# Layer 1's neighbour sums: 26 groups of sixteen chunks and two scattered quartets per half group, in place of 21 groups and three quartets

## What is computed

```
row, col = (edge_index[0], edge_index[1])          # row = src, col = dst
agg = segment_sum(x[col], row, num_segments=3125)
h = (1.0 + eps) * x + agg
h = h @ W1.T + b1
... batch normalisation over the nodes, ReLU ...
return h @ W2.T + b2
```

## Time and profile before

| | |
|---|---|
| median of the runs | 7078.2 us |
| span of the profiled execution | 8961.2 us (27% above the median) |
| TensorE matmul busy in the span | 5673.7 us (63%) |
| VectorE busy | 4867.9 us (54%) |
| GpSimd busy | 4865.9 us (54%) |
| ScalarE busy | 1151.3 us (13%) |
| mean granted TensorE clock | 0.674 of full |
| stage that the change touches | 4725 to 5720 us of the span |

### The profile page before, as it was taken

The page is one execution under the profiler, slowest core; times in us unless marked ns, Lnnn a source line. Parts: engine busy times, 40 slices in busy tenths (PEclk is TensorE's granted clock), DMA queues, the critical chain, the costliest instruction groups (busy, mean ns, idle before and its releaser), DMA issues. The chain is left out here.

```text
span 8961.2 us, 134318 instructions
## 1 busy us (share of the span) xinstructions
PE 5673.7 (63%) x28658; PEld 4800.1 (54%) x28659; DVE 4867.9 (54%) x17338; ACT 1151.3 (13%) x3238; POOL 4865.9 (54%) x4715
## 2 busy tenths in 40 slices
PE   6555556677777767777768778656666665333334
PEld 5555555466666556666655555456666663333333
DVE  6555554455555545555557777545555553444555
ACT  1111111111111111111112222100000001000001
POOL 2566564555555355555527888445454451566664
PEclk6555555777777877777779999865655556555556
DMA  5334434333333233333324444333333332333332
GB/s 154 95 95 97 94 94 126 92 97 93 95 93 96 57 102 94 94 97 98 94 53 67 69 69 69 78 83 88 89 89 87 89 89 37 77 75 75 74 77 49
DMA packets 930244, 770.85 MB, mean 86 GB/s; under 512 B 586631, under 2 KB 762899, under 8 KB 928115
## 3 DMA queue, kind: packets, MB, share of 16 engines
q0 software_dynamic: 245936, 426.87, 19.9%
q1 hardware_dynamic: 675276, 329.60, 14.6%
q10 hardware_dynamic: 8960, 13.52, 0.6%
HBM read 681.88 MB, written 86.32 MB: 86 GB/s over the span
## 5 line engine op out<-in xcount | busy, mean ns | idle before, releaser
L1180 POOL DMA_INDIRECT there<-table_wide,idx x1664 | 1597.4, 960 | 1396.8 <-DVE prod L1203 615.9
L1271 PE MATMUL ps<-here,hot_t 128*128 x3328 | 1238.1, 507 | 631.3 <-DVE there L1222 599.7
L2288 POOL DMA_INDIRECT there<-table_wide,idx x832 | 792.7, 953 | 902.6 <-DVE msg L2364 434.8
L1222 DVE TENSOR_TENSOR there<-there,ps 128x512 f32<-128x512 f32 x832 | 571.2, 687 | 1169.8 <-remote 607.7
L1271 PEld LDWEIGHTS ps<-here,hot_t 128*128 128x128 f32 x3328 | 740.9, 247 | 756.5 <-issue 668.9
L2677 POOL DMA_INDIRECT there<-table_narrow,idx x832 | 791.3, 951 | 649.5 <-issue 259.1
L693 POOL DMA_INDIRECT rec<-out_recd,posd x806 | 817.5, 1014 | 564.4 <-issue 263.9
L1279 PE MATMUL ps<-relu,hot_s 128*128 128x128 f32 x3328 | 878.0, 356 | 140.3 <-DVE hot_s L1211 108.1
L2837 PE MATMUL ps<-here,hot_t 128*128 x1664 | 434.5, 436 | 803.6 <-DVE prod L2758 419.3
L1947 POOL DMA_INDIRECT partial_sums<-row_sums1a,idx1a x504 | 814.9, 1617 | 167.4 <-issue 147.3
L1279 PEld LDWEIGHTS ps<-relu,hot_s 128*128 128x128 f32 x3328 | 688.5, 238 | 326.3 <-issue 272.1
(11 more groups left out here) (486 smaller groups left out, 9773.3 us busy)
## 6 DMA issues: line engine op xcount, KB each, us to landing
locrows<-loc_row SPq DMA_DIRECT2D x416, 256.0 KB
krowd<-key_row SPq DMA_DIRECT2D x201, 256.0 KB
there<-table_wide,idx POOLq DMA_INDIRECT x2496
src_rows1a<-slot_src_row SPq DMA_DIRECT2D x42, 768.0 KB
lrowd<-lo_row SPq DMA_DIRECT2D x201, 128.0 KB
attr_raw<-in_edge_attr SPq DMA_DIRECT2D x201, 128.0 KB
there<-table_narrow,idx POOLq DMA_INDIRECT x832
rec<-out_recd,posd POOLq DMA_INDIRECT x806
```

Source lines behind the costliest of these rows:

```text
L1180: nc.gpsimd.indirect_dma_start(there[:, j, q, :], None, table, bass.IndirectOffsetOnAxis(idx[:, j, q:q + 1], 0)).then_inc(gathered[j][q], 16)
L1222: nc.vector.tensor_tensor(pair, pair, ps[:, WORK, :], ALU.add).then_inc(summed, 1)
L1271: last = nc.tensor.matmul(ps[:, WORK, (q % 2) * 2 * F:(q % 2 + 1) * 2 * F], hot_t[:, j % 2, q * P:(q + 1) * P], here[:, :, :].rearrange("p ...
L2288: nc.gpsimd.indirect_dma_start(there[:, j, q, :], None, table, bass.IndirectOffsetOnAxis(idx[:, j, q:q + 1], 0)).then_inc(gathered[j][q], 16)
```

## The change

The three numbers of the layout change (26 groups of sixteen dense chunks, so 52 half groups, with 8 scattered chunks each: 416 dense and 416 scattered places, 832 in all), and what served the third quartet goes from each engine's order: `match` 2 on VectorE, `count` 2 and the late `total` on TensorE, `keep` 2 and the late `take` on ScalarE. `QUADS` is worked out from `SPARSE` and becomes 2, and with it GpSimd's loop has 8 scatters per half group.

```diff
 GROUP = 16
-GROUPS = 21
-SPARSE = 12
+GROUPS = 26
+SPARSE = 8
 DENSE = GROUP * GROUPS
 SLOTS1 = DENSE + 2 * SPARSE * GROUPS
 TILES1 = -(-NV // P)
@@ VectorE, step
                 line(i, h, (2, 3), first)
                 if h == 0:
                     locate(i, 2, first)
-                match(i, h, 2)
                 shift(i, h)
                 line(i, h, (4, 5), first)
                 place(i, h, first)
@@ ScalarE, step
                     take_tally(i, h, first and h == 1)
                     if h == 1:
                         own_rows(i)
-                        take(i, 0, 2, first)
-                    else:
-                        take(i - 1, 1, 2, False)
                 keep(i, h, 0, opening)
                 keep(i, h, 1, opening)
                 take(i, h, 0, first)
-                keep(i, h, 2, False)
                 take(i, h, 1, first)
@@ ScalarE, end
             take_tally(GROUPS, 0, False)
-            take(GROUPS - 1, 1, 2, False)
@@ TensorE, step
                 opening = first and h == 0
-                if not opening:
-                    before = blocks_at(half(i, h, SPARSE) + (DENSE - 4), 4)
-                    if h == 1:
-                        fetch(i, first)
-                        total(i, 0, 2, before, False)
-                    else:
-                        total(i - 1, 1, 2, before, False)
+                if h == 1:
+                    fetch(i, first)
                 mine = blocks_at(half(i, h, SPARSE) + DENSE, 8)
                 count(i, h, 0, opening)
                 count(i, h, 1, opening)
@@
                     if v == 3:
                         total(i, h, 0, mine[0:4], opening)
-                    if v == 7:
-                        count(i, h, 2, False)
                     if v == 9:
                         total(i, h, 1, mine[4:8], False)
@@ TensorE, end
-            total(GROUPS - 1, 1, 2, blocks_at(SLOTS1 - 4, 4), False)
             for t in range(4):
                 multiply(GROUPS, 0, t, False)
```

## The result

The changed kernel takes 7000.1 us (four runs, 6995.53 to 7004.93) against 7077.95 us before; the ratio is 0.9884, 95% interval 0.9870 to 0.9898. That is 78 us less by the medians (72 to 92 by the interval). Forecast were 40 us and 7038 us, in a range of 6980 to 7150: the sign and the range held, and the size was half of what came.

What follows compares the result with a forecast made beforehand. GpSimd was taken to bound the stage; afterwards 51 half groups of 17.9 us (912.9 us) plus 7.2 us end it at 5672.0 in place of 5712.6, 40 us less: 7038 us, range 6980 to 7150.

Steps and rivals of the forecast that it cites:

- GpSimd paces the stage of before: The stage before the change: GpSimd's 504 scatters at 1.92 us each set its length, while TensorE and VectorE have slack.
- GpSimd stops pacing with 8 scatters per half group: The changed stage: 8 scatters at 1.92 us take 15.4 us per half group, below what TensorE and VectorE need.
- TensorE's floor of 16.7 us: TensorE's half group falls from 17.1 to 16.7 us; ScalarE's four copies still hold up visit 0.
- VectorE sets h = 0 at 18.3 us: VectorE's h = 0 half group: 19.7 us from the opening less 1.4 us for `match` 2 and a shorter `target`.
- The clock's term of 0.9 us a pair: TensorE's clock falls after one of two idle stretches at `multiply` 1, making a pair 0.9 us longer; bounds 0 and 1.7.
- The rival of a quicker GpSimd: Unrecorded scatters quicker than 1.84 us make the change a loss: 7149 us at 1.70 us, 7224 at 1.52; chance 0.28.
- The rival of lines that lock GpSimd out: VectorE's sixteen one-hot lines of 0.69 us stop GpSimd for their whole length: 25.8 us a half group, 7452 us; chance 0.02.
- The small things: Wider `src_upper` costs under 0.5 us; ScalarE's dropped copy pair and layer 0's chunk sorting nothing; SP's loads costed at nothing.

Runs made afterwards that it cites:

- experiment 5: The changed kernel with VectorE's four one-hot matrices of destinations per group moved to where VectorE waits for a multiply: 6986.8 us, ratio to before 0.9867.
- experiments 6 and 7: The changed kernel with the second quartet's total at the next half group's head: 6963.6 us; the same plus destination one-hot matrices moved to VectorE's waits: 6935.1 us.
- experiment 2: The kernel before with only the first two quartets of each half group scattered, 336 scatters in place of 504: 6870.4 us, ratio to before 0.9696.
- experiment 3: The changed kernel with four more VectorE comparisons per half group, where the third match stood, into an unread buffer: 7019.4 us, ratio to before 0.9903.
- experiments 2 to 8: Besides those with their own lines: 4, the changed kernel unedited, 6992.4 us; 8, the changed kernel without scatters or waits for them, 6987.3 us.
- experiment 1: The kernel before, unedited, recorded a second time: span 7089.0 us, time 7091.1 us; the first record spanned 8961.2 us.

## Why the prediction was right in its direction, and wrong in its size

- **GpSimd paces the stage of before:** right. Taking a third of the scatters away and nothing else made the stage 211 us shorter.
- **GpSimd stops pacing with 8 scatters per half group:** right. Eight at 1.68 + 0.30 us are 15.8 us of 16.98 (15.4 were forecast, from the shorter scatters of before), and it waits for rows now.
- **TensorE's floor of 16.7 us:** right, 16.83 in experiment 5, with the reason given for it (ScalarE's copies hold up visit 0), which experiments 6 and 7 show.
- **VectorE sets h = 0 at 18.3 us: this step failed.** It took 19.7 us from one half group of the opening and took 1.4 off. The 1.4 were about right: from experiment 2 to the changed kernel h = 0 went from 18.80 to 17.50, 1.3 us, and experiment 3 has the match at 1.09. The start was not: in the steady loop of the same kernel, not held up by GpSimd, it is 18.80 (experiment 2), 0.9 less. About half of that, 19.72 - 19.19 = 0.5 us, comes with the third quartet's scatters, between the same half group of both kernels: VectorE's lines took 700 ns on average there with them, between 4755 and 4776 us, and 656 without. The other 0.4 us separate the loop's first h = 0 from the later ones in experiment 2 itself, with lines as long (657); why is open. So a half group from the opening was no sample of a loop in which GpSimd has slack. h = 1 was forecast at TensorE's 16.7 and measures 16.45, as it follows a late `add` 0. The pair is 0.8 + 0.25 us shorter than forecast, 33.95 us in place of 35.0: 25.5 pairs x 1.05 = 27 us.
- **The clock's term of 0.9 us a pair: this step failed too, it is nothing.** It was made of one fall behind one of two idle stretches, and of a wait of `multiply` 1 of 1.6 us in each pair. That wait isn't there: in the loop of the changed kernel TensorE never waits for `dense` by the record (2.3 us in all, at the end). The clock is at 2.4 GHz (1.00) through the whole loop of the changed kernel and of experiments 2 to 8, also where TensorE waited up to 1.5 us for `dense` (experiment 2). 25.5 x 0.9 = 23 us. Together with the 27 they are 50 us, and 47.5 with the prediction's rounding of 17.95 to 17.9 us a half group taken off. That is what lies between the forecast and the record: from the first scatter to the end of the last work, 927.7 us were forecast (5672.0 - 4744.3), and it is 4498.67 - 3618.55 = 880.1.
- The Trainium skill, TensorE: Matmul & The Clock Gate, section "HAM oscillation — how this bites in real kernels", has the clock fall when TensorE idles, and by that rule the changed kernel should hold it. The trace agrees: 0.90 before, 1.00 after. The prediction named the rule and gave nothing for it; here the rule was the better guide than the two stretches counted.
- **The rival of a quicker GpSimd, given 0.28: wrong.** A second record shows 1.93 us a scatter in an execution as long as the runs. The reasoning behind it (that 1883 of the 2777 us that were not GpSimd's pace could hardly vanish) was a sound sum from a record that should have been distrusted: they did vanish. In the stretches of experiment 1 gathers went from 1.74 to 1.26 us apart, which is the 0.95 + 0.30 us that the prediction had as GpSimd's own pace.
- **The rival of lines that lock GpSimd out: no.** Scatters went from a mean of 1617 to 1682 ns with half as many lines again per scatter (two in place of 1.33), so 0.065 us, not 16 x 0.69 us in eight. The Trainium skill, SBUF — State Buffer, section "Who interferes with whom", has the second to come, of GpSimd and a VectorE operation in a two-port mode, wait for the whole length of the first. In these traces the mean line is 10 to 65 ns longer than the 635 without scatters, and the mean scatter 0.08 (before) to 0.14 us (after) longer than the 1.54 of a scatter beside an idle VectorE. Single ones come nearer to it: the longest two of the 504 scatters of before are 2.17 and 2.21 us, longer by about one line, while the longest line, 0.97 us, is longer by 0.34 us and not by a scatter.
- **The small things** (loads, ScalarE, the wider `src_upper`): right, none shows.

## What to carry to other kernels

When an engine that paced a loop gets slack, the others' new pace should be taken from a stretch, or a run, in which it has slack: the opening of this loop showed who comes next, but slower than they were later (19.7 us a half group in place of 18.8). A half group that follows a late one measures short; judge two alternating halves by their sum. Time taken off or put on an engine that has waits counts only as far as the waits don't take it up (experiment 3: 2.2 us of work in a pair, 1.2 us of time). And work is free where an engine waits for a copy at the head of a step: that place is worth filling first, here with 0.9 us of TensorE per half group.

## What was not expected

A recorded execution was 27% longer than its kernel's runs while GpSimd's indirect DMAs took as long as ever, within 4%; the changed kernel's record and the second of before lie within 0.2% of their runs. A stage's length can still be right in such a record (994.9 and 997.1 us here), and which stages were disturbed showed only against a second one.
